# Second attention: where ScalarE's evacuations of turned chunks stand among its counts

## The reference, cut to what matters

```python
draft = jnp.einsum('bhqd,bhkd->bhqk', qr, kr)
draft = draft + jnp.where(causal_future, neg, 0.0)
num_remain = max(min(Sq, MIN_REMAIN), Sq - int(Sq * MASK_OUT))   # 128
_, draft_indices = jax.lax.top_k(draft, num_remain)
mask = mask.at[b_idx, h_idx, s_idx, draft_indices].set(0.0)
scores = jnp.einsum('bhqd,bhkd->bhqk', qr, kr) / np.sqrt(HD) + mask
attn = jax.nn.softmax(scores, axis=-1)
out = jnp.einsum('bhqk,bhkd->bhqd', attn, v)
```

## Time and profile before

| what | value |
|---|---|
| median of three runs | 5202.4 us |
| the profiled execution, its own time | 5201.94 us |
| span of the profiled execution | 5200.1 us |
| ScalarE busy | 2818.0 us (54%) |
| VectorE busy | 3264.8 us (63%) |
| TensorE busy | 4071.3 us (78%) |
| mean granted clock of TensorE | 0.852 of full speed |
| slots of the second attention (L1240) | 32, from 2189.6 to 4714.7 us |

### The profile page before, as it was taken

One profiled execution on the slowest core, in us unless ns is written; L12 is line 12 of the kernel. 1 busy time (PEld: TensorE's weight loads), 2 busy tenths in 40 slices (PEclk: granted clock), 3 DMA queues, 4 the chain that ended last, 5 costly groups with the idle time before them and its releaser, 6 DMA issues. The chain is left out here.

```text
span 5200.1 us, 84202 instructions
## 1 busy us (share of the span) xinstructions
PE 4071.3 (78%) x25610; PEld 2336.7 (45%) x25752; DVE 3264.8 (63%) x9571; ACT 2818.0 (54%) x6546; POOL 313.2 (6%) x1173
## 2 busy tenths in 40 slices
PE   6998999998999999646767466766667667675899
PEld 2445666665444444323434233434334344343454
DVE  3556777775333355577776777777777767776344
ACT  1114777774000011278777478778777777877100
POOL 1000000000000000001101001111011010110000
PEclk8999999999999999858767677778777777776899
DMA  4236232322111123301110110111101111010442
GB/s 143 69 76 165 61 78 55 77 69 96 49 48 48 46 63 76 68 21 27 24 24 6 23 27 4 26 27 26 25 4 27 27 27 23 4 27 6 114 117 78
DMA packets 308435, 260.33 MB, mean 50 GB/s; under 512 B 188672, under 2 KB 242704, under 8 KB 307920
## 3 DMA queue, kind: packets, MB, share of 16 engines
q1 hardware_dynamic: 307376, 254.32, 19.2%
q0 software_dynamic: 544, 0.07, 0.0%
HBM read 176.21 MB, written 78.12 MB: 49 GB/s over the span
## 5 line engine op out<-in xcount | busy, mean ns | idle before, releaser
L1072 ACT ACTIVATE a_sign<-arena,a_state 128x384 fp8e4<-128x384 f32 (+5 forms) x1056 | 917.7, 870 | 141.9 <-DVE a_state L1279 98.0
L967 PE MATMUL a_ps_s<-k,q 128*128 128x512 bf16 (+3 forms) x1474 | 447.4, 439 | 674.0 <-DVE arena L1342 452.9
L1038 ACT ACTIVATE a_probT<-a_ps_t 128x512 f32<-128x512 f32 (+3 forms) x768 | 364.1, 481 | 372.8 <-PE a_ps_t L986 360.1
L967 PEld LDWEIGHTS a_ps_s<-k,q 128*128 128x128 bf16 x1536 | 154.3, 122 | 875.5 <-DVE arena L1342 504.2
L979 PE MATMUL a_ps_t<-ident,arena 128*128 128x128 f32 x1584 | 345.6, 337 | 175.2 <-ACT a_probT L1038 137.1
L1072 ACT ACTIVATE a_sign<-a_third,a_state 128x384 fp8e4<-128x384 f32 (+2 forms) x480 | 417.3, 871 | 100.6 <-DVE a_state L1279 95.4
L738 ACT ACTIVATE a_prob<-a_x_neg,a_shift 128x640 f32<-128x640 f32 (+7 forms) x512 | 397.1, 776 | 88.0 <-DVE a_x_neg L781 63.4
L1005 PE MATMUL a_ps_o<-a_probT,vals 128*64 128x128 f32 x4608 | 395.2, 314 | 49.8 <-ACT a_probT L1038 49.8
L781 DVE TENSOR_SCALAR_CACHE_REDUCE a_x_neg<-a_ps_s 128x640 f32<-128x640 f32 (+7 forms) x512 | 378.8, 751 | 41.7 <-PE a_ps_s L662 26.6
L677 PE MATMUL a_ps_t<-ident,a_prob 128*128 128x128 f32 x2304 | 365.0, 282 | 35.4 <-issue 13.0
L1290 DVE MAX8 a_nine<-a_below 128x8 f32<-128x256 f32 (+6 forms) x448 | 371.1, 828 | 34.5 <-issue 1.8
(11 more groups left out here) (263 smaller groups left out, 6929.8 us busy)
## 6 DMA issues: line engine op xcount, KB each, us to landing
q<-qk SPq DMA_DIRECT2D x256, 256.0 KB, 4.6
qk<-p_qkT SPq DMA_DIRECT2D x32, 960.0 KB, 6.2
h_rows<-h SPq DMA_DIRECT2D x32, 512.0 KB, 6.9
k<-qk SPq DMA_DIRECT2D x256, 64.0 KB, 5.0
h<-tok_h SPq DMA_DIRECT2D x16, 512.0 KB, 4.0
arena<-in_wo SPq DMA_DIRECT2D x16, 512.0 KB, 9.1
o<-a_o SPq DMA_DIRECT2D x16, 512.0 KB, 2.7
q<-o SPq DMA_DIRECT2D x16, 512.0 KB, 5.7
```

What stands on the lines that cost most here:

```text
L967: nc.tensor.matmul(ps_s[:, n % 2, a:a + w], q[:, y, head, i * P:(i + 1) * P], k[:, y, a:a + w], start=(y == 0), stop=False, skip_group_che ...
L1038: nc.scalar.activation(probT[:, n % 4, 0:w], ps_t[:, (n + 1) % 2, 0:w], ACT.Exp).then_inc(probT_ready, 1)
L1072: ins = nc.scalar.activation(to, xs[mine][:, at:at + w], ACT.Sign, scale=-1.0, saturate=False, bias=state[:, par, 0, n:n + 1], accum_out=s ...
```

## The change

It touches two things. The 40 units of BETWEEN are now added at steps 14 and 28, so that they stand behind each count and none ahead of the first. And `count(p)` no longer starts with evacuations and a drain ahead of its wait for the limits: the chunks of a pass's first step are emitted behind the wait, at the short tile.

```diff
-                    counted = [sum(2 + i for _, i in (RANKED * EVAC_PASSES)[:k] if i > 1) + BETWEEN * ((k + NS - 1) // NS)
+                    counted = [sum(2 + i for _, i in (RANKED * EVAC_PASSES)[:k] if i > 1) + BETWEEN * (k // NS)
                                for k in range(EVAC_PASSES * NS + 1)]
...
                     def count(p):
 
-                        evacs(p * NS)
-                        if p == 0:
-                            act.drain()
                         wait_alone(act, t_ready, s * PASSES + (p + 1), const_in, 48)
                         for n, (m, i) in enumerate(RANKED):
                             at, w = ps_seg(m, i), (i + 1) * P
                             if n in SHORT:
                                 if n:
                                     act.drain()
-                                    evacs(p * NS + n)
+                                evacs(p * NS + n)
                                 continue
```

## The result

The change made the kernel faster, by twice what was forecast: 5084.81 us (median of four runs, 5081.01 to 5090.8) against 5199.9 us (four runs of before on the same chip, 5194.66 to 5205.07). The ratio is 0.977, 95% interval 0.9755 to 0.9785. The forecast of 5143 us and its whole range, 5092 to 5192, lie above. The profiled execution took 5084.22 us.

The account below looks back on a forecast made before the run. A loop between ScalarE's counts and VectorE's narrowings was taken to bound each slot. A, B and C summed to 50.3 against 52.14 us; with clock and loop-turn terms 1.95 us per slot, 30 slots, 58.5 us: 5143 us, range 5092 to 5192.

Parts of the forecast that it names:

- A: From a slot's first limits (L1240) to the start of its first narrowing (L1253): 15.3 us forecast, 21.52 before.
- the loop turns: Three turns of the loop over slots, where VectorE's start stalls 3 us: A is 14.0 + 3, costing 0.2 us per slot.
- the 58.8 us that it took off for slot 8: One exact selection on VectorE in slot 8, subtracted from 2394.1 us to get 80.5 us per slot.
- the new A is mostly counting and doesn't follow: Claim that A no longer lengthens where the clock rises later, saving another 0.5 us per slot.
- B: From the first narrowing's start to the second's: 19.8 us forecast, 2.2 more than before; 23.7 with the block at 1.2 GHz.
- The block: Six chunks, 8 to 13, evacuated in a row behind the first count: 6.8 us at 2.4 GHz, 10.7 at 1.2 GHz.
- six hand-overs: Term between ScalarE and TensorE in the six-chunk block, raising its 6.0 us to 6.8.
- I keep that share: Seven slots with a long B at low clock stay seven, each now adding 3.9 us, not 3.1: 0.2 us per slot more.
- The clock is late more often: Rival: low clock in B in 15 to 20 slots, not 7, 3.9 us each: 5174 to 5194 us; chance 0.20.
- The rival of a low clock in every slot: Clock stays low in the six-chunk block and second count: 75 us lost, 5277 us; chance 0.10.
- C: From the second narrowing's start to the third's: 15.2 us forecast, 2.1 more than before, its end passing from ScalarE to VectorE.
- The rival in which TensorE keeps up: No waits in A, VectorE's floor of 14.0 sets it: 39 us more saved, 5104 us; chance 0.17.

Follow-up runs that it names:

- the run without a second block: Changed kernel with chunks 0 and 1 ahead of the first wait for the limits, units between second and third count left out: 5145.96 us, ratio 0.9896.
- the 24 transposes: 24 extra TensorE transposes ahead of chunk 0: in before 5146.23 us, in after 5058.36 us, in the version with two chunks ahead of the wait 5044.16 us.
- the move alone: After with the old table, so the first step's six chunks stand behind the wait for the limits but ahead of the first count: 5237.21 us, ratio 1.0052.
- the two new orders: After (5084.81 us), and the new table with chunks 0 and 1 ahead of the first wait for the limits (5035.85 us), both without added transposes.

## Why the prediction was right in direction and wrong in size

**A: right.** 15.5 us was forecast with the loop turns, 15.75 measured. The waits were 1.36 us in slot 3 for the 1.6 forecast, ahead of chunk 4 and chunk 6 as it said. The ordinary slot's A is 15.83, 0.5 longer than the 15.3 forecast, with the clock at 0.50 nearly all through; at the three loop turns it is 16.8, not 17. What the forecast had too small is the old mean of the three pieces, 53.48, where it reckoned 53.3: the 58.8 us that it took off for slot 8 hold more than the exact selection, for that slot's C is 68.00 where others have 13.1, 54.9 more, and its B is a long one. The step "the new A is mostly counting and doesn't follow" the clock holds roughly: A was 0.9 us shorter where the clock stood at 0.77 and not at 0.50.

**B: the step that failed.** Forecast 20.7 on average (19.8, and 3.9 in seven slots), measured 18.98. The block was put at 6.8 us, "with six hand-overs" of 0.8 in it. It is 5.65: the term was mis-sized by 1.15 us. 0.8 of this are the hand-overs. From the values of chunk 8 on TensorE goes on without waiting: 1.02, 1.14 and 1.19 us from start to start, and 0.10 us behind the last ScalarE is at chunk 13. So the hand-overs that there are, of about 0.1 us each, are within the 5.65, and the 0.8 came on top of a sum that needed none. The other 0.35 us are in its terms: durations of rows, which are some 0.1 longer than the time to the next start, and turns of 1.3 and 1.2 where 1.14 and 1.19 were measured. With 0.2 us elsewhere that is 19.8 against 18.45 in slots like slot 3. Slots like slot 7 have 19.5: TensorE, at 1.2 GHz until then, comes to the block about a microsecond behind. The second part of the failure is "I keep that share": the seven slots are those in which the clock fell back and the block ran at 0.50, and in the changed kernel it fell back ahead of the block in none. Of the 0.9 us that this share was to add to the mean, 0.5 is seen, and it has another source, a clock that rises late: 12 slots of 30 with 1.0 to 3.4 us each over 18.45. That is the place of the rival "The clock is late more often", at a lower price than its 3.9. The rival of a low clock in every slot fell: in 26 of 30 slots the block ran at 1.00 from its start. The Trainium skill's rule behind it (TensorE: Matmul & The Clock Gate, "A second HAM failure mode: psum-queue depth-cycling") has a swing between the two levels from the limits to the second narrowing in 13 of 30 slots before the change, not only in the seven that the prediction counted, and in 1 after it, although six waits of ScalarE for TensorE, and of TensorE for ScalarE, now follow one another in each. With seven in a row (the run without a second block) it has 8 of 30.

**C: the mechanism was wrong, the size nearly right.** Forecast 15.2 with VectorE ending it, measured 14.56. The four chunks took 4.0 us, as forecast, and the first fetch came 5.95 us behind the count, as forecast (6.0). But VectorE's work from there to the end of the copy was 8.5 us, not 8.8 + 0.3: a wait of 0.3 us on scores was in the 8.8 already, and one of 0.26 us for GpSimd was gone. So it was done 0.25 us ahead of ScalarE, and ScalarE ends C as it did before: 4.0 + 10.6.

**The sum.** Saved per slot 4.19 us, forecast 1.95. Of the 2.24 between, B gives 1.7, C 0.64, the mean of before 0.18, and A takes back 0.25. Thirty times 4.19 is 125.7 us, against 58.5 forecast; 8 of it are lost again outside these pieces, 6.8 behind the third narrowing of slot 31. The rival in which TensorE keeps up named 5104 us, nearest to the result, but by the wrong place: A isn't at 14.0.

**What stays open.** Why the clock falls back within A in the old order and not in the new one. It did so in the three traces with six chunks ahead of the first count and without the 24 transposes (before 12 slots of 30, the move alone 22, eight transposes at chunk 5 16), and in no slot of the eight other traces without them. With the 24 transposes the clock was up early and fell back within A in either order (22 slots in before, 25 and 26 in the two new orders). So the order makes the difference, but no run separates what it is in it: just ahead of the fall in slot 6 of before TensorE was busy 3.92 of 5.00 us, and it was busy 3.92 in the like stretch of slot 3, where nothing fell. It also stays open why the clock rises late in some slots of the changed kernel, and why it was lower in slots 32 and 33.

## What to carry to other kernels

Where an engine both closes a search loop and drains another's buffers, put drains that are ready into its wait for the loop, and the others between its loop work, as far apart as the slower engine needs; one expression of a table was worth 2.9% here, and the wrong place for one or two ready chunks gave 0.6 to 0.9% back. When a block of hand-overs is priced from a timeline, take start-to-start times, and add a hand-over only where one engine waits for the other. And price the same order at either clock before calling a gain or a loss one of the clock.

## What the runs showed of the hardware

More work on TensorE, on the path, did not make the kernel before slower: with eight transposes per slot it took 0.9974 of its time (0.996 to 0.9987), and with 24 it was faster, 0.9872 (0.985 to 0.9895). The granted clock over the whole of A rose from 0.72 on average to 0.83 in both, and the faster turns behind paid for them. The same 24 bring nothing once ScalarE waits for the turns for less than 1 us in A (0.9703 with, 0.9685 without, intervals overlapping).

A fall of TensorE's clock costs by where it ends. In before it fell back within A in 12 slots: where it was up again ahead of the block B was 17.6, and where the block ran at 0.50 B was 20.6 to 20.7, 3.1 us more; with seven chunks in the block (the run without a second one) it was 26.2 against 21.9. So the clock is to be read slot by slot: the mean over A was lower in the faster kernel, 0.61 against 0.72.
